# The filter over the width as one plain float32 product

## The reference

```python
xs = jnp.einsum('bhwc,dc->bhwd', x, W1) + b1       # 768 -> 192 channels
xs = jax.nn.gelu(xs, approximate=False)
xs = fft_low(xs)      # |inverse FFT of the masked FFT|, over h and w
xs = jnp.einsum('bhwd,cd->bhwc', xs, W2) + b2      # 192 -> 768 channels
return x + xs
```

## Time and profile before

| | |
|---|---|
| median of 3 runs | 2202.89 us (2202.61 to 2204.13) |
| profiled execution | 2201.8 us, span 2200.0 us |
| TensorE busy | 2142.0 us, 97% |
| VectorE busy | 1623.7 us, 74% |
| ScalarE busy | 1114.4 us, 51% |
| GpSimd busy | 327.5 us, 15% |
| DMA | 707.40 MB, mean 322 GB/s |

### The profile page before, as it was taken

How to read it: one execution, slowest core, us unless ns; L and a number is a source line. 1 busy time by engine, 2 the same in 40 slices (tenths; PEclk the granted TensorE clock), 3 DMA queues, 4 the chain that set the end, 5 groups by cost and what they waited for, 6 DMA issues and landing times.

```text
span 2200.0 us, 37824 instructions
## 1 busy us (share of the span) xinstructions
PE 2142.0 (97%) x12512; PEld 1939.0 (88%) x12512; DVE 1623.7 (74%) x2380; ACT 1114.4 (51%) x1861; POOL 327.5 (15%) x500
## 2 busy tenths in 40 slices
PE   6899999999999999999999999999999999999998
PEld 5799988989899898988989889998898989989876
DVE  6768687686877868778686776868768687786846
ACT  4565454645445555454554546545464544555532
POOL 1311111111111111111111111111111111111100
PEclk9999999999999999999999999999999999999999
DMA  6789988898888988988889888998889889888878
GB/s 209 234 304 350 347 316 306 322 361 335 302 325 322 345 322 314 344 317 329 333 319 350 316 320 318 351 344 314 305 322 363 332 293 334 325 342 324 317 291 344
DMA packets 253758, 707.40 MB, mean 322 GB/s; under 512 B 84242, under 2 KB 150930, under 8 KB 249620
## 3 DMA queue, kind: packets, MB, share of 16 engines
q1 hardware_dynamic: 253716, 706.86, 86.1%
HBM read 455.12 MB, written 251.66 MB: 321 GB/s over the span
## 4 chain that ended last, share of the span: by engine, by line
PE 92%; ACT 3%; DVE 2%; issue 1%; DMA 1%; SPq 0%; DVEq 0%; ACTq 0%
PE ps_h L277 24%; PE ps_h L278 11%; PE ps_o L341 8%; PE ps_o L338 8%; PE ps_o L335 8%; PE ps_o L332 8%; PE ps_o L331 8%; PE ps_o L316 8%; PE ps_f L288 2%; PE ps_o L310 2%; PE ps_f L290 2%; PE ps_f L289 2%; DVE xlo L464 1%; ACT xhi L372 1%; DMA rows_b<-filt 1%
## 5 line engine op out<-in xcount | busy, mean ns | idle before, releaser
L277 PE MATMUL ps_h<-w1s,xhi 128*128 128x384 f32 x3072 | 899.7, 361 | 25.0 <-DVE xlo L464 24.3
L278 PE MATMUL ps_h<-w1s,xlo 128*128 128x192 f32 x3072 | 770.9, 251 | 0.0
L277 PEld LDWEIGHTS ps_h<-w1s,xhi 128*128 128x128 f32 x3072 | 579.2, 189 | 42.5 <-DVE xlo L464 17.7
L511 DVE TENSOR_TENSOR xo<-ps_o,xo 128x1024 f32<-128x1024 f32 x384 | 470.3, 1225 | 178.5 <-PE ps_o L341 174.5
L278 PEld LDWEIGHTS ps_h<-w1s,xlo 128*128 128x128 f32 x3072 | 588.7, 192 | 7.6
L390 ACT ACTIVATE filt<-ps_f 128x384 f32<-128x384 f32 x256 | 126.2, 493 | 799.6 <-PE ps_f L290 799.2
L464 DVE TENSOR_TENSOR xlo<-xin,xhi 128x1536 fp32r<-128x1536 f32 x256 | 450.4, 1759 | 3.9 <-ACT xhi L372 3.9
L575 POOL TENSOR_TENSOR diff<-hid 128x192 f32<-128x192 f32 x240 | 166.8, 695 | 1462.6 <-ACT hid L381 1460.6
L372 ACT ACTIVATE xhi<-xin 128x1536 fp32r<-128x1536 f32 x256 | 377.8, 1476 | 8.2 <-DMA xin<-xt_dram 7.9
L473 DVE TENSOR_TENSOR hid<-ps_h,b_rows 128x192 f32<-128x192 f32 x512 | 181.0, 354 | 185.4 <-PE ps_h L278 183.1
L341 PE MATMUL ps_o<-ob,w2b_hi 128*128 128x512 f32 x768 | 303.4, 395 | 1.0 <-DVE ob L502 1.0
(11 more groups left out here) (52 smaller groups left out, 2056.6 us busy)
## 6 DMA issues: line engine op xcount, KB each, us to landing
xin<-xt_dram SPq DMA_DIRECT2D x256, 768.0 KB, 7.3
xo<-xt_dram SPq DMA_DIRECT2D x128, 1536.0 KB, 12.2
out_dram<-xo SPq DMA_DIRECT2D x128, 1536.0 KB, 8.6
rows_a<-filt SPq DMA_DIRECT2D x256, 128.0 KB, 5.2
cols_a<-rows_a SPq DMA_DIRECT2D x64, 512.0 KB, 3.7
rows_b<-filt SPq DMA_DIRECT2D x256, 64.0 KB, 6.2
cols_b<-rows_b SPq DMA_DIRECT2D x64, 256.0 KB, 4.2
xo<-w1t_dram SPq DMA_DIRECT2D x1, 576.0 KB, 4.5
```

The source lines that it names most:

```text
L277: nc.tensor.matmul(ps_h[tt][:, 0:2 * D], hi, w1s[:, k, :], start=k == 0, stop=False)
L278: ins = nc.tensor.matmul(ps_h[tt][:, D:2 * D], lo, w1s[:, k, 0:D], start=False, stop=k == KC - 1)
L511: nc.vector.tensor_tensor(x, ps_o[u % 2][:].rearrange("p (j a n) -> p j a n", j=2, a=2), x, ALU.add).then_inc(s_add, 1)
```

## The change

gelu_pair writes hid alone, in plain float32. hid_hi, hid_lo, hid_lo_pair and the semaphore s_hlo are gone, and so is the split of the filter matrix in the head: fw is loaded as it is. filter_w_pair is one plain float32 product of 384 columns that waits for s_gelu. Since that product reads hid itself, hid_tile waits for s_f before it writes a pair's first tile into the buffer; gelu_pair no longer waits for it.

```diff
-        fw_hi = sb("fw_hi", [P, P], F32R)
-        fw_lo = sb("fw_lo", [P, P], F32R)
+        fw = sb("fw", [P, P])
...
-        hid_hi = sb("hid_hi", [P, 2, 2, D], F32R)
-        hid_lo = sb("hid_lo", [P, 2, 2, D], F32R)
...
-                sp.dma_start(fwf, filter_w).then_inc(s_const, 16)
+                sp.dma_start(fw[:], filter_w).then_inc(s_const, 16)
...
-                pe.wait_ge(s_hlo, PAIRS * i + q + 1)
+                pe.wait_ge(s_gelu, PAIRS * i + q + 1)
                 if q >= 1 or later(i):
                     pe.wait_ge(s_fs, PAIRS * i + q)
-                hi, lo = (m[:, q % 2, :, :].rearrange("p t d -> p (t d)") for m in (hid_hi, hid_lo))
-                nc.tensor.matmul(ps_f[:, 0:2 * D], fw_hi[:], hi, start=True, stop=False)
-                nc.tensor.matmul(ps_f[:, 0:2 * D], fw_lo[:], hi, start=False, stop=False)
-                nc.tensor.matmul(ps_f[:, 0:2 * D], fw_hi[:], lo, start=False, stop=True).then_inc(s_f, 1)
+                nc.tensor.matmul(ps_f[:, 0:2 * D], fw[:], hid[:, q % 2, :, :].rearrange("p t d -> p (t d)"), start=True, stop=True).then_inc(s_f, 1)
...
-                if q >= 2 or later(i):
-                    act.wait_ge(s_f, PAIRS * i + q - 1)
                 pre = hid[:, q % 2, :, :]
-                nc.scalar.activation(hid_hi[:, q % 2, :, :], pre, ACT.Gelu)
                 nc.scalar.activation(pre, pre, ACT.Gelu).then_inc(s_gelu, 1)
...
                     dve.wait_ge(s_acc, PAIRS * i + t // 2 - 1)
+                    dve.wait_ge(s_f, PAIRS * i + t // 2 - 1)
...
-            def hid_lo_pair(i, q):
-                dve.wait_ge(s_gelu, PAIRS * i + q + 1)
-                if q >= 2 or later(i):
-                    dve.wait_ge(s_f, PAIRS * i + q - 1)
-                nc.vector.tensor_tensor(hid_lo[:, q % 2, :, :], hid[:, q % 2, :, :], hid_hi[:, q % 2, :, :].bitcast(F32),
-                                        ALU.subtract).then_inc(s_hlo, 1)
...
-                link(nc.vector.tensor_copy(fw_hi[:], fwf))
-                nc.vector.tensor_tensor(fw_lo[:], fwf, fw_hi[:].bitcast(F32), ALU.subtract)
...
-                hid_lo_pair(0, 0)
                 hid_tile(0, 2)
                 xlo_pair(0, 2)
                 hid_tile(0, 3)
-                hid_lo_pair(0, 1)
...
-                    if here is not None:
-                        hid_lo_pair(*here)
```

More of the change, by code:

```diff
@@ L94, in lowpass_kernel @@
         w2af, w2bf, b2f = scratch[:, 1, 0:C], scratch[:, 2, 0:C], scratch[:, 3, 0:C]
-        fwf, cornerf = scratch[:, 4, 0:P], scratch[:, 5, 0:8 * P].rearrange("p (b n) -> p b n", b=2)
+        cornerf = scratch[:, 5, 0:8 * P].rearrange("p (b n) -> p b n", b=2)
         ps_h = [ctx.enter_context(nc.psum_tensor(f"ps_h{n}", [P, 512], F32)) for n in range(2)]
@@ L114, in lowpass_kernel @@
         s_gelu = sem("gelu_done")
-        s_hlo = sem("hid_lo_ready")
         s_f = sem("filtered_w")
```

## The result

The changed kernel takes 2206.53 us (median of 19 runs, 2203.26 to 2212.72), the kernel before 2201.99 us on the same chips (19 runs, 2200.78 to 2205.44); the ratio is 1.0022, 95% interval 1.0015 to 1.0029. So it is slower by 4.5 us, where I had forecast +2.1 and "no change that can be told". That is inside the range, but the interval leaves out 1, and 4.5 is just over the 4.4 that I had set as the edge of what can be told. Measured again later, beside other experiments, the same kernel stood at 1.0016 (1.0007 to 1.0025), +3.3 us.

The account below looks back on a forecast made before the run. TensorE was taken to bound turns 1 to 15, something else turn 0. Product +30.1, stall -21.5 and turn 0 -6.5 sum to +2.1 us on the 2202.89 median: 2205.0 us, range 2200.5 to 2213.

Parts of the forecast that it names:

- no change that can be told: Forecast verdict for the whole kernel: +2.1 us, under the 4.4 us (0.2%) a measurement can tell; chance 0.60.
- The price of the product: TensorE's filter product: one plain product 0.671 us against 0.545 for three rounded; 0.126 over 239 steps, +30.1 us.
- L296's row over L316's: Plain record of 384 columns priced from L296 (192 columns) at 0.323 us, not from L316 (128 columns) at 0.334.
- its weight load is what holds it: Reason for setting L316 aside: a 128-column product with a full weight load each time is likelier held by that load.
- The rival that priced a column by the rounded products: Filter product at 0.350 us a record, 0.180 more a step: sum +15.0, 2217.9 us; chance 0.06.
- count of four passes: Skill's rule that true FP32 takes four array passes against three; at the rounded pace it would give 2217.9 us.
- The wait that goes: TensorE's stall for VectorE's hid_lo at step 4 of turns 1 to 15: 1.44 us each, -21.5 us used.
- wait for ob or for an add: Rival: the step 4 stall stays under another name, at the output unit or next add; +21.5, 2226.5 us; chance 0.04.
- the margin: At step 4, ob complete at 275.71, needed by the output unit's fifth product at 276.6: 0.9 us to spare.
- Turn 0: Steps shorten from 4.99 to 4.56 us, 6.0 us over 14 steps, plus 0.5 in the head: -6.5 us.
- a dearer record: Rival: plain product dearer per column in 239 steps, so slower; chance 0.28 (0.22 about 2210, 0.06 about 2218 us).
- One bound of the range: Whole kernel's lower bound, 2200.5 us, said to be turn 0 at its best and a record of 0.320.

Follow-up runs that it names:

- the order alone: Kernel before with only hid_lo(5) moved ahead of split_lo(0) on VectorE at step 3 of every full turn: 2179.89 us, ratio 0.9902.
- the later pair: Traces of the kernel before and the changed kernel, each with TensorE's wait for the last add moved from a map's first to third bank: spans 2197.8 and 2201.5.
- both tails shortened: Kernel before and changed kernel, each with the wait at the start of turn 16 moved to a map's third bank: 2200.17 us (0.9994) and 2203.82 us (1.0007).

## Why the prediction was right, and where it was off

**The price of the product.** Forecast 0.126 us a step, +30.1. Measured 0.128 by the turns and by the distances over two products, +30.6. The choice of L296's row over L316's was right: the three pieces of 128 columns show that a short record costs more for each column. That its weight load is what holds it, as I argued, no run shows. The rival that priced a column by the rounded products (0.180 a step) is out. So is what the Trainium skill's count of four passes ("FP8 and Floating Point Precision", section TensorE Precision Notes), priced at a rounded pass, would have given. If each of the two records is two passes, which fits but which no run shows by itself, then by the 0.667 a plain pass is cheaper than a rounded one, some 0.32 us for two over 384 columns against 0.175 for one.

**The wait that goes.** Forecast -21.5; the traces give 1.44 us a turn and the order alone -22.0 in the median. No wait for ob or for an add took its place in the full turns of any kernel without it; how wide the margin is, forecast as 0.9 us, no run measured.

**Turn 0.** Forecast -6.5. The first trace has -6.7, the later pair -5.6. That the figure came so near is in part luck, since two errors were opposite. The step fell to 4.46 us where I had said 4.56, which over 14 steps is 7.3 us and not 6.0. And I had named only what frees the step and not what it runs into next: the load of x behind read_cols on SyncE, some 1.8 us by the traces. What is left from step 1 on is 5.1 to 5.4. The rest is the head and the first step, for which I gave 0.5 and the two pairs of traces have 1.6 and 0.2. Over all kernels the old turn 0 ends between 106.1 and 107.3 (four traces), the changed kernel's between 99.9 and 100.6 (three).

**The sum.** +2.1 was forecast; the medians give +4.5, +3.3 and, with both tails shortened, +3.65. Turns 1 to 15 were forecast at +8.6 (30.1 less 21.5) and are +9.0 and +9.3 in the two pairs of traces. Turn 0 was forecast at -6.5 and is -6.7 and -5.6. In the later pair these two are the whole difference of 3.7 us. In the first pair 1.5 us more come from a stretch at half clock in turn 16; that the changed kernel meets such stretches oftener than the one before I have not shown, and with that wait shortened the difference was 3.65, between the two measured without. So the term that is not settled is the head and first step of turn 0, which move by a microsecond between traces of the same code; how it is spread over the runs stays open. It is also why the sign of a change worth 0.1 to 0.2% was harder to tell than its parts: errors of 1 us and less moved the total from "same" to just over the edge of 4.4, where I had given 0.32, and not for the reason that I had put behind those 0.32, a dearer record.

One bound of the range doesn't come out of its terms: turn 0 at 8 and a record at 0.320 take 1.5 and 1.4 us off 2205.0, which is 2202.1 and not 2200.5. The result lies above both.

## What to carry to other kernels

When an edit takes work off an engine that isn't the bound, look for the one wait in the bound engine that ends on that work, and ask first whether its place in the order is to blame: here moving one instruction gave 22 us, and the change that deleted the instruction gave the same and paid 30 for it. Price a product by a row of its own kind, and of two such rows take the one whose column count is nearer; a plain float32 product of 384 columns costs 0.67 us against 0.545 for three rounded ones. A dearer form is free where the engine has room, so let it run there alone, and then ask what the shorter step runs into. And look at how much code a loop holds: here six records in place of two added twelve waits of 2 us and the half clock behind some of them.

## What the runs showed of the hardware

- A plain float32 product of 384 columns with 128 columns of weights shows as two records. In the changed kernel it takes 0.667 to 0.673 us; three rounded ones take 0.545. In three pieces of 128 columns, six records, it takes 0.687 us. Behind a plain product the next product's start is drawn some 0.3 us early (0.37 after L283), so distances must be taken over both.
- TensorE's granted clock fell to 1.2 GHz, half of 2.4, for a stretch behind a wait, in some executions and not in others of the same wait: behind the wait of 2.63 us at the start of turn 16 in six of the nine traces that have it, behind a wait of 2.26 us in turn 0, behind 1.44 us in turn 16 in two traces, and behind five of twelve waits of some 2 us at the end of a turn. The first trace paid 1.5 us for one.
- Code that a loop turn fetches anew: 135 packets on the instruction queue in place of 25, and twelve waits of 1.8 to 2.4 us at the twelve jumps back.
